# Attention on one core: the sums of each head gathered by transfers, inverted once a half, and spread through DRAM as factors

## The reference

```python
scores = jnp.einsum('bhqd,bhkd->bhqk', q, k) / jnp.sqrt(jnp.float32(hd))
scores = jnp.where(causal, scores, -jnp.inf)
weights = jax.nn.softmax(scores, axis=-1)
attn = jnp.einsum('bhqk,bhkd->bhqd', weights, v)
```

## Time and profile before

| | |
|---|---|
| median of 3 runs | 1865.74 us (1859.0 to 1866.49) |
| span of the profiled execution, first to last instruction | 1852.8 us |
| its own time | not listed beside the span; the runs lie 6.2 to 13.7 us above it |
| instructions in the span | 49530 |
| PE / PEld busy | 92% / 73% |
| DVE / ACT / POOL busy | 78% / 53% / 57% |
| DVE RECIPROCAL L917 | 256 of them, 182.0 us |
| POOL L1008 and L1023 | 64 of each, 63.2 and 63.4 us |

### The profile page before, as it was taken

How to read it: one execution, slowest core, us unless ns; L and a number is a source line. 1 busy time by engine, 2 the same in 40 slices (tenths; PEclk the granted TensorE clock), 3 DMA queues, 4 the chain that set the end, 5 groups by cost and what they waited for, 6 DMA issues and landing times. The chain is left out here.

```text
span 1852.8 us, 49530 instructions
## 1 busy us (share of the span) xinstructions
PE 1700.5 (92%) x14718; PEld 1360.0 (73%) x14719; DVE 1437.1 (78%) x3985; ACT 976.7 (53%) x2048; POOL 1056.0 (57%) x1446
## 2 busy tenths in 40 slices
PE   5899999999999999999999998589999986988883
PEld 4677777777777777777777775368888876877773
DVE  4589899999999899899999996378888971455554
ACT  1166666666676666666666765333444422544441
POOL 4045555555555655655555556446777770567666
PEclk8899999999999999999999999679999997999996
DMA  2555556556556555555565453223333356999996
GB/s 76 80 132 152 141 128 158 142 119 166 141 135 144 147 147 138 135 154 142 123 162 141 123 147 99 109 74 105 126 120 120 122 155 169 286 327 326 323 331 220
DMA packets 226548, 291.13 MB, mean 157 GB/s; under 512 B 57142, under 2 KB 188954, under 8 KB 226458
## 3 DMA queue, kind: packets, MB, share of 16 engines
q1 hardware_dynamic: 190042, 186.14, 40.3%
q0 software_dynamic: 18048, 49.31, 8.2%
q10 hardware_dynamic: 18368, 54.64, 7.7%
HBM read 83.25 MB, written 129.69 MB: 115 GB/s over the span
## 5 line engine op out<-in xcount | busy, mean ns | idle before, releaser
L752 ACT ACTIVATE probs<-bank 128x376 f32<-128x376 f32 (+2 forms) x896 | 440.7, 529 | 272.9 <-PE bank L621 261.0
L843 DVE TENSOR_REDUCE neg_max<-bank 120x1 f32<-120x376 f32 (+2 forms) x896 | 507.0, 587 | 53.7 <-PE bank L587 49.7
L587 PE MATMUL bank<-k_rows,q_rows 64*128 64x128 f32 (+2 forms) x1536 | 403.7, 345 | 3.1 <-ACT probs L752 2.4
L621 PE MATMUL bank<-q_rows,k_rows 64*120 64x120 f32 (+2 forms) x1536 | 369.9, 336 | 3.9 <-ACT probs L752 3.6
L982 POOL TENSOR_SCALAR_AFFINE_SELECT probs<-probs 128x512 f32<-128x512 f32 (+1 forms) x384 | 232.4, 631 | 209.5 <-ACT probs L752 209.3
L604 PE MATMUL bank<-causal,own_row 56*120 56x56 bf16 (+4 forms) x1792 | 300.9, 248 | 8.7 <-DMA k_rows<-k_flat_hi 3.5
L587 PEld LDWEIGHTS bank<-k_rows,q_rows 64*128 64x128 f32 (+1 forms) x1536 | 246.2, 186 | 6.7 <-ACT probs L752 4.6
L2205 POOL DMA_INDIRECT y_got<-y_sorted,p_route x188 | 182.4, 970 | 119.7 <-issue 117.6
L621 PEld LDWEIGHTS bank<-q_rows,k_rows 64*128 64x128 f32 (+1 forms) x1536 | 229.8, 183 | 8.7 <-ACT probs L752 5.8
L604 PEld LDWEIGHTS bank<-causal,own_row 64*128 64x128 bf16 (+2 forms) x1792 | 153.4, 115 | 110.3 <-DVE neg_max L843 39.9
L1847 POOL DMA_INDIRECT x_sorted<-r_normed,route x188 | 184.3, 981 | 83.6 <-issue 59.0
(11 more groups left out here) (235 smaller groups left out, 4148.8 us busy)
## 6 DMA issues: line engine op xcount, KB each, us to landing
x_sorted<-zeros ACTq DMA_DIRECT2D x32, 816.0 KB, 3.8
y_sorted<-zeros ACTq DMA_DIRECT2D x32, 816.0 KB, 4.3
x_rows<-x_sorted SPq DMA_DIRECT2D x51, 512.0 KB, 6.4
y_sorted<-p_y_rows SPq DMA_DIRECT2D x51, 512.0 KB, 6.4
q_rows<-q_flat_hi SPq DMA_DIRECT2D x256, 94.0 KB
k_rows<-k_flat_hi SPq DMA_DIRECT2D x248, 94.0 KB
q_rows<-q_flat_lo SPq DMA_DIRECT2D x128, 94.0 KB
out_dram<-base SPq DMA_DIRECT2D x47, 256.0 KB, 5.0
```

Of the source, the lines that this page charges most:

```text
L587: last = eng.matmul(ps[0:T[t], m * w:(m + 1) * w], q[rows, slot, t * P:t * P + T[t]], k[rows, slot, 0:w], start=False, stop=(m == len(head ...
L621: last = eng.matmul(ps[0:T[t], m * w:(m + 1) * w], k[64 * c:64 * c + 64, slot, t * P:t * P + T[t]], q[64 * c:64 * c + 64, slot, t * P:S], ...
L752: eng.activation(probs[g % 2][0:T[t], first:first + len(heads), OFF[t]:OFF[t] + w], bank_exp[n % 2][0:T[t], 0:len(heads) * w].rearrange("k ...
L843: eng.tensor_reduce(dst, src, AX.X, ALU.max, negate=True).then_inc(max_taken, 1)
```

## The change

ACT keeps each product once, whole (`heads_of[half][e]`, a buffer for each half). SP gathers from it one partition of each strip of sums: two transfers for a half, each taking 4 partitions of 376 values to 32 partitions of 47 values. DVE inverts 64 partitions of 47 values in one instruction, at unit 10 (half 1) and unit 23 (half 0), after a wait for the gathering transfers. SP writes the inverses to DRAM (two transfers), waits for them, and loads them back with each row repeated on 16 partitions (two transfers that fill 128 partitions of 376 values each); the rows in between are zeros, cleared once in DRAM, so that the product with the factors drops what isn't an output. POOL multiplies even and odd, adds them and splits the sum as before. `join`, the shuffle and the scales of ACT are gone.

```diff
-        sums_swapped = sb("sums_swapped", [P, S])
-        sums = sb("sums", [P, S])
-        recip = sb("recip", [P, S])
+        PIECE = S // 8
+        sums = [sb(f"sums{h}", [8 * 8, PIECE]) for h in range(2)]
+        inverse = [sb(f"inverse{h}", [8 * 8, PIECE]) for h in range(2)]
+        inverse_dram = nc.dram_tensor("inverse_rows", [2, 2, 8, S], F32, kind="Internal").ap()
+        inverse_of = [sb(f"inverse_of_{e}", [P, S]) for e in ("even", "odd")]
...
-                    eng.activation(sum_of[e][:, :], bank_pv[:, 0:S], ACT.Copy, scale=strip_half[:, 1 - e:2 - e])
-                    eng.activation(attn_of[e][:, :], bank_pv[:, 0:S], ACT.Copy, scale=strip_half[:, e:e + 1])\
+                    eng.activation(heads_of[half][e][:, :], bank_pv[:, 0:S], ACT.Copy)\
                         .then_inc(odd_kept if e else even_kept, 1)
...
-                HALF_1_AT = {10: (0, 1), 12: (2,), 14: (3,), 16: (4,)}
-                HALF_0_AT = {21: (0,), 23: (1, 2), 25: (3,), 26: (4,)}
+                HALF_1_AT, HALF_0_AT = 10, 23
...
+                def invert_sums(st, half, shift):
+
+                    eng.wait_ge(sums_gathered[half], st.at(shift, 32, 32))
+                    eng.reciprocal(inverse[half][:, :], sums[half][:, :]).then_inc(recip_done, 1)
...
-                    eng.tensor_tensor(attn_raw[:, :], attn_raw[:, :], recip[:, :], ALU.mult).then_inc(attn_scaled, 1)
+                    eng.wait_ge(recip_loaded, st.at(shift, 64, 32 * (half + 1)))
+                    even, odd = heads_of[half]
+                    eng.tensor_tensor(even[:, :], even[:, :], inverse_of[0][:, :], ALU.mult).then_inc(scaled_even, 1)
+                    eng.tensor_tensor(odd[:, :], odd[:, :], inverse_of[1][:, :], ALU.mult).then_inc(scaled_odd, 1)
...
+                    eng.tensor_tensor(attn_raw[:, :], even[:, :], odd[:, :], ALU.add).then_inc(attn_scaled, 1)
...
+                def gather_sums(st, half, shift):
+
+                    wait_alone(eng, even_kept, st.at(shift, 2, half + 1), passed_sp)
+                    wait_alone(eng, odd_kept, st.at(shift, 2, half + 1), passed_sp)
+                    for e in range(2):
+                        first = 16 * (1 - e)
+                        eng.dma_start(sums[half][32 * e:32 * e + 32, :], heads_of[half][e][first:first + 97:32, :])\
+                            .then_inc(sums_gathered[half], 16)
+
+                def spread_inverse(st, half, shift):
+
+                    wait_alone(eng, recip_done, st.at(shift, 2, half + 1), passed_sp)
+                    if isinstance(st.i, int) and st.b + shift == 0 and half == 0:
+                        eng.wait_ge(inverse_cleared, 16)
+                    for e in range(2):
+                        eng.dma_start(bass.AP(inverse_dram.tensor, (16 * half + 9 * e) * S, [[2 * S, 4], [1, S]]),
+                                      inverse[half][32 * e:32 * e + 32, :]).then_inc(recip_stored[half], 16)
+                    if not (isinstance(st.i, int) and st.b + shift == 0 and half == 0):
+                        wait_alone(eng, attn_scaled, st.at(shift, 2, half), passed_sp)
+                    wait_alone(eng, recip_stored[half], st.at(shift, 32, 32), passed_sp)
+                    for e in range(2):
+                        eng.dma_start(inverse_of[e][:, :], bass.AP(inverse_dram.tensor, (16 * half + 8 * e) * S,
+                                                                   [[S, 8], [0, 16], [1, S]])).then_inc(recip_loaded, 16)
...
                 def step(st):
                     if st.attend:
                         max_rows(st, 1, 0)
+                    if st.finish:
+                        gather_sums(st, 1, -1)
+                        spread_inverse(st, 1, -1)
                     if isinstance(st.i, int) and st.real == B - 1:
                         load_experts(st)
                     if st.front:
                         rows(st, 0, "q")
                         if not opening(st):
                             rows(st, 0, "k")
+                    if st.attend:
+                        gather_sums(st, 0, 0)
                     if st.maxima:
                         max_rows(st, 0, 1)
+                    if st.attend:
+                        spread_inverse(st, 0, 0)
                     if st.finish:
                         store(st)
```

More of the change, by code:

```diff
@@ L195, in attention_phase @@
         odd_kept = sem("odd_kept")
-        joined = sem("joined")
-        sums_ready = sem("sums_ready")
+        scaled_even = sem("scaled_even")
+        scaled_odd = sem("scaled_odd")
+        inverse_cleared = sem("inverse_cleared")
+        sums_gathered = [sem(f"sums_gathered{h}") for h in range(2)]
         recip_done = sem("recip_done")
+        recip_stored = [sem(f"recip_stored{h}") for h in range(2)]
+        recip_loaded = sem("recip_loaded")
         attn_scaled = sem("attn_scaled")
@@ L733, in keep @@
                     half, e = g // 2, 1 - g % 2
[L734 to L735 removed]
+                    if not (isinstance(st.i, int) and st.b + shift == 0):
+                        eng.wait_ge(attn_scaled, st.at(shift - 1, 2, half + 1))
                     eng.wait_ge(pv_done, st.at(shift, GROUPS, g + 1))
[L737 to L738 removed]
+                    eng.activation(heads_of[half][e][:, :], bank_pv[:, 0:S], ACT.Copy)\
                         .then_inc(odd_kept if e else even_kept, 1)
@@ L942, in step @@
                             take_lo(st, f"nT{j}", nT[st.b % 2][1][:, j, :], nT[st.b % 2][0][:, j, :])
-                        if st.finish and n in HALF_1_AT:
-                            for piece in HALF_1_AT[n]:
-                                gather_sums(st, 1, -1, piece)
+                        if st.finish and n == HALF_1_AT:
+                            invert_sums(st, 1, -1)
                         if st.front and n in (13, 15):
@@ L951, in step @@
                                 take_lo(st, f"k{j}", k_flat[1][:, j, :], k_flat[0][:, j, :], bias=bias_k[:, j:j + 1])
-                        if st.attend and n in HALF_0_AT:
-                            for piece in HALF_0_AT[n]:
-                                gather_sums(st, 0, 0, piece)
+                        if st.attend and n == HALF_0_AT:
+                            invert_sums(st, 0, 0)
                         if st.mix and n == 27:
@@ L1013, in normalise @@
                     eng.tensor_tensor(lo, attn_raw[:, :], hi.bitcast(F32), ALU.subtract).then_inc(attn_done, 1)
[L1015 to L1020, removed]
-                    eng.wait_ge(even_kept, st.at(shift, 2, half + 1))
-                    eng.wait_ge(odd_kept, st.at(shift, 2, half + 1))
-                    eng.tensor_tensor(attn_raw[:, :], attn_of[0][:, :], attn_of[1][:, :], ALU.add)
-                    eng.tensor_tensor(sums_swapped[:, :], sum_of[0][:, :], sum_of[1][:, :], ALU.add)\
-                        .then_inc(joined, 1)
                 def residual(st):
@@ L1053, in step @@
                                 mask(st, g, t)
-                        if g == 0 and st.finish:
-                            join(st, 1, -1)
                         if g == 1 and st.finish:
                             normalise(st, 1, -1)
-                        if g == 1 and st.attend:
-                            join(st, 0, 0)
                         if g == 3 and st.maxima:
```

19 lines of the change are left out of this document (5 added, 14 removed).

## The result

The kernel after takes 2260.86 us (median of 4 runs, 2254.88 to 2268.63), the kernel before 1865.95 us in the same session; the ratio is 1.2121, interval 1.2089 to 1.2154. That is slower, as forecast, but 173 us above the 2088 and outside the range. The profiled execution took 2254.88 us, its span is 2253.1 us.

A forecast was written before the change was run, and what follows sets the result against it. PE and DVE were nearly full, and SP's serial list was to set the step: 29 steps of 41.0 instead of 34.04 us (+203), +5 before step 1, +14 at the end, +222 on 1865.7 gives 2088 us; range 1970 to 2190.

The forecast's parts named there:

- both land 3.8 after the issue: SP's loads of half 1: issued 18.1 to 19.4 into the step, the last landing at 18.75 + 3.8 = 22.5 us.
- The clock: Behind PE's hole at the output projection: half clock for 5 us loses nothing or 2.3 us a step; 1.0 taken.
- Rival 3: PE's clock falls in every step, 2.3 instead of 1.0 us: 2126, up to 2180 with later load landings; chance 0.22.
- The issues: SP's list: twelve more transfer issues a step at 0.65 us each with gap, and four waits.
- SP's list decides: SP's serial list sets the step: the next `rows(1)` starts at 40.0 us instead of 34.04, before the clock's loss.
- The two chains: To the next `rows(1)`: PE alone from its output projection gives 38.3 us, SP's list gives 40.0.
- DVE's relief: DVE gets 5.6 us a step back; PE can keep no more than 1.2 us of it.
- Rival 2: DVE's relief decides: transfers fit in SP's air, PE's 1.2 us of waits go each step; 1835 us, chance 0.03.
- Rival 4: No visible change: the new waits cost what DVE's relief gives; 1866 us, chance 0.03.
- The signs named ahead: Step 39 to 43 us, q wait under 1, DVE gap about 2, PEld waiting 4 for `attnT`, PE share about 85.
- the sign of "wrong": Wrong if SP has air ahead of `rows(0)`, loads land before 20 us, or PE's longest wait is for maxima.
- dear bound: Issues at 0.75, 1 us more on three landings, 2.3 for the clock: step 46.5 us, +380, 2246 us.

The follow-up runs named there:

- e9_clears_late: The changed kernel with ACT's two clears issued in units 21 and 24 instead of 14 and 16; 2168.9 us, ratio 1.1631.
- e5_none2: The changed kernel without its transfers and inversions, POOL multiplying by a constant, so the output is not the attention's; 1863.66 us, ratio 0.999.
- e12_16_late: `e9_clears_late` with each inverse row stored twice and loads reading 16 rows repeated 8 times; 2169.26 us, ratio 1.1638.
- e4_clears: The changed kernel with ACT's two clears issued in units 1 and 4 instead of 14 and 16; 2197.15 us, ratio 1.1759.
- e2_half0: The changed kernel gathering, inverting and spreading half 0 alone, half 1 multiplied by half 0's factors; 2056.5 us, ratio 1.1007.

## Why the prediction was wrong

**The sum over the whole.** The same instruction of steps 1 and 30 stands at 134.01 and 1491.49 after, which is 46.81 us a step (34.04 before). 29 x 12.77 = 370 us; 7.7 more before step 1 and 22.3 more behind step 30 (761.6 against 739.35 us to the end of the span). Forecast were 203, 5 and 14. Of the 178 us missed on the span, 29 x (46.81 - 41.0) = 168 are the step.

**The step, term by term.** The loop in the prediction's own terms, for the kernel after (from 648.09) and for `e9_clears_late` (from 613.39):

| us | forecast | after, this step | after, mean of 25 | late clears, this step | late clears, mean of 25 |
|---|---|---|---|---|---|
| R to the issue of the second load of half 1 | 18.75 | 17.85 | 18.2 | 18.29 | 18.3 |
| to POOL's first multiplication | 3.75 | 9.48 | 8.7 | 4.16 | 5.2 |
| to PE's output projection | 5.2 | 4.98 | 5.0 | 5.05 | 5.0 |
| to DVE's inverse of half 0 | 5.0 + 1.0 clock | 7.06 | 7.9 | 6.22 | 7.0 |
| to the next R | 7.3 | 7.40 | 7.4 | 8.84 | 8.3 |
| step | 41.0 | 46.77 | 47.2 | 42.56 | 43.8 |

R is SP's first issue of `rows(1)`, where a step starts. The means are over the 25 steps that start from 134 to 1265 us after and from 134 to 1183 us with late clears, read from the same timelines; after, the last steps are shorter, so that the mean over 29 is 46.81. Both steps shown are on the quick side, that of the late clears above all.

- *The step that failed* is "both land 3.8 after the issue". It was the landing of the clears themselves, taken for a load of 192 KB "just ahead of" which one clear goes. Two clears of 816 KB went out, one ahead of the loads and one 0.5 us behind the issue of the last, then thirteen transfers of `rows(0)`, and the load took 9.48. What came was a landing while the DMA share stood at 1.01 (666 to 668). In the mean 5.0 of the 6.2 us missed a step stand in that row. In this step it is 5.7 of 5.8, but only because an earlier issue (0.9) and a dearer clock (1.1) cancel.
- *The clock* cost 2.1 in this step (7.06 against 4.98 in the earlier trace rows, where the clock was 1.00: 632.19 - 627.21), 3.3 in 19 of the 25 and 2.9 in the mean, and not 1.0. This is the second term that was too small. Rival 3 had 2.3 in each step, which was the better guess. The Trainium skill's rule (TensorE: Matmul & The Clock Gate, "HAM oscillation — how this bites in real kernels") that each wait for a transfer in a loop throttles anew is borne out here: the stretch was longer than 4.98 in each of the 25 steps. Rival 3's range of 2126 to 2180 still stopped short, as it took a landing of 4.1.
- *The issues* were right: 0.56 to 0.62 with gaps of 0.05, where 0.65 was taken; twelve and four waits in SP's list; gathers 1.75 us from the second issue to the reciprocal (660.40 to 662.15), taken 2.2. The reciprocal is 0.44 (taken 0.45), POOL's five operations 4.9 (taken 5.0).
- *"SP's list decides"* was wrong: SP waits for the inverse 5.9 us in this step (682.05 to 687.99). The loop runs through SP, the landing, POOL, PE's hole and DVE's half 0, and back to SP; no list is full. The two chains that the prediction set side by side (38.3 and 40.0) are one.
- *DVE's relief* was right in size (4.8 us a step by the busy totals, (1437.1 - 1284.8) / 32, against 5.6) but for PE it is worth nothing that can be measured, and not "up to 1.2": `e5_none2`. Rival 2 (faster, 1835) fell by that kernel alone: without any transfer it would still have been 1864. Rival 4's premise, that the relief is worth something, fell with it.
- *The signs named ahead*: no air ahead of q, as said; the gap at unit 10 was 1.08 and not 2; PE's wait 9.13 and not 4; PE's share 80.7 and not 85. The loads landed at 27.3 from R and not 22.5; the sign of "wrong" looked for them below 20, on the other side.

The measured time is above even the prediction's own dear bound (2246 us, a step of 46.5), which its range left out. That bound comes near the step by other terms: dearer issues and 1 us more on each of three landings, where the issues were cheaper and one landing was 5 us dearer.

With the clears elsewhere half of the error goes (92 of 173 us), and the step is still 2.8 us above the forecast in the mean: 1.4 in the landing, which goes with the thirteen transfers behind it and with its 8 rows (3.3 in `e12_16_late`), 1.0 in the clock and 1.0 in the last row, where the clears now meet the stores, less 0.7 in the other two. That a kernel without clears would reach 41.0 wasn't tried, since the later stages read what they clear. Nor was one clear moved without the other: how the landing of 9.2 to 9.6 divides between them and `rows(0)` rests on the comparison of steps above.

## What to carry to other kernels

Before a load with a waiting engine behind it is priced, list what every other queue issues from a few us ahead of it to a few us behind, with its bytes: the landing of the same load took 3.7 to 6.1 us or 9.2 to 9.6 here, and that, once a step, was most of the error. Look at many steps before a landing is called typical: neighbours differ by 1.5 us for a start of the next transfers that differs by 1. A round trip through SP, DRAM and back (two gathers, two stores, two loads) took 15.6 us from first issue to use in half 1 (659.79 to 675.42) and 11.8 with late clears (median; 10.7 in the step shown, 625.11 to 635.84); it needs a consumer that much later, on every engine that stands behind it, and not just a free engine at its end. And ask first what the relieved engine gives: one run with the work left out (`e5_none2`) showed that 16 points of a 91% busy DVE were worth nothing.

## What the runs showed of the hardware

- A load of 192 KB issued between two transfers of 816 KB on another queue, the second of them 0.3 to 0.5 us behind it, landed after 9.2 to 9.6 us; with the second 1.0 to 1.7 us behind it, after 4.9 to 5.6; the DMA share was 1.01 from 666 to 668.
- Without such a transfer near, the same load landed after 3.7 to 4.4 us when the next transfers on its own queue started 1.6 us or more behind it, and after 5.2 to 6.1 when they started 1.1 us behind (`e9_clears_late`, 23 of 25 steps).
- Issuing takes longer near the 816 KB transfers: two issues of 1.27 to 1.34 us took 2.00 (stores, `e9_clears_late`), 2.28 (`e4_clears`) and 2.45 (`rows(0)` at 667.31 in the kernel after) on SP.
- The same bytes from 16 rows in place of 8 landed 0.9 us sooner with four transfers behind (medians 3.9 and 3.0) and 2.1 us sooner with thirteen (5.4 and 3.3).
- Half clock followed a PEld wait of 2.45 us (`e2_half0`: six loads took 1.57, and 0.84 at full). 28 matmuls without a use in a hole of 9 us brought the stretch behind it from 7.9 to 5.3 us in the mean (4.98 at full clock).
